# Middle blocks of a five-layer network: deeper lags in the quantised feed-forward, both halves mixed per step in the recurrence, output weights mixed by diagonals on TensorE

## The chip, the cores and the metric

The kernel runs on one core of a Trainium2 chip. The metric is the device time of one execution in microseconds; the figure for a kernel is the median of its runs.

## What is computed

`h` starts as the output of a token attention over looked-up embeddings (16 heads), a spin attention is added to it, and then come the three parts that matter here, cut to their core. `h` has 2 sequences of 1024 tokens, 256 wide.

```python
# L0_ffn: fake-quantised activations and weights, scale from the largest absolute value
xq   = quant(layernorm(h), clip_x)
hid  = quant(silu(xq @ qw(w_gate).T) * (xq @ qw(w_up).T), clip_down)     # 704 wide
h    = h + hid @ qw(w_down).T
# L1_attn: 8 experts' weights are mixed once per sequence, then a gated linear recurrence
u     = layernorm(h)
x     = u * rsqrt(mean(u*u) + 1e-6) * norm_weight
probs = softmax(mean(x, axis=1) @ router_w.T + router_b)                 # [2, 8]
W_hg, W_out = einsum('be,ekd->bkd', probs, w_hg), einsum('be,eod->bod', probs, w_out)
hidden, gate = split(x @ W_hg.T)
state_t = (1 - sigmoid(gate)) * state_(t-1) + sigmoid(gate) * g(hidden)
h    = h + (state @ W_out.T + u)
# L1_ffn: six layers of windowed attention and gated feed-forward on layernorm(h)
h    = h + L1_ffn(layernorm(h))
```

## The kernel before

The program is a row of blocks with a barrier of all engines between them: `attentions` (both attentions and the quantisation of the weights), `feed_forward`, `recurrence`, `local_layers` (six layers, 96 tile steps) and `store_sum`. Only `feed_forward` and `recurrence` are touched by the change. Within a block each engine has a queue of its own whose order is written out by hand, and semaphores tie them together. Tokens are cut into 4 chunks of 512 (`CHUNKS`) and 8 pairs of 128-token tiles (`PAIRS`); PSUM has 8 banks of 128x512 float32.

**`feed_forward`, gates.** VectorE clips `X` in two operations per chunk (`clip_x`, L1515 and L1517), ScalarE rounds it to bf16 (`round_x`, L1453), TensorE turns it (`turn`, L1384), ScalarE takes it back (`take_x`). Then come 6 units per chunk: TensorE makes gate and up (`gate_up`, L1394, three bank pairs), ScalarE applies Silu (`gated`, L1465), VectorE multiplies (`multiply`, L1523) and takes the largest of each half (`largest`, L1530). `clip_x` of chunks 2 and 3 stands inside VectorE's loop, at `j == 4` of chunks 0 and 1. GpSimd first clears the tail of `hT` (L1335), then sets `power` and `ones`.

**`feed_forward`, down projection.** Once the largest value is known, each of 8 pairs `g` goes through this chain: `to_integers` (ScalarE, L1469), `clip_h` (VectorE, L1536), `round_h` (ScalarE, L1474), `down` (TensorE, L1404), `scale_output` (VectorE, L1541), `add_output` (GpSimd, L1346), `count` (VectorE, L1547 and L1550), `deviations` (GpSimd, six small operations), `norm` (VectorE, L1555), `join` (GpSimd, L1367) and `norm_again` (ScalarE, L1482), `turn_normed` with the sums (TensorE, L1414 and L1421), `take_normed` (VectorE, L1560). VectorE's order in step `g` is:

```python
clip_h(g); count(g - 1); scale_output(g); norm(g - 1); take_normed(g - 3)   # and near the end:
mean_of(0)  # at g == 6;   logits(0)  # at g == 7;   shares(0)  # at g == 8
```

After the loop stand `mean_of(1)`, `logits(1)` and `shares(1)`. `shares` also writes `shareT`, the shares times the norm's weight (L1588).

**`recurrence`.** VectorE mixes the gate weights of a unit `n` (sequence, 128 outputs) from 8 experts: `mix(n)` has 16 operations of 128x256, two (k = 0, 1) per expert (L1770, L1773). TensorE multiplies (`hidden_gate(n)`, L1703, 8 float32 matmuls of 512 columns, which the profile shows as 16 records), ScalarE takes three sigmoids (L1742 to L1744), VectorE scans (`scan(n)`, L1778, L1781, L1783), in the order mix 0, 1, 2, scan 0, mix 3, scan 1, 2, 3. The output weights are mixed beside it: ScalarE scales each expert's (`weigh_output`, L1737) and GpSimd adds them up (L1684), 7 additions per sequence. Then TensorE makes the outputs of 8 pairs (`output`, L1718, 4 float32 matmuls of 256 columns each, 8 records), VectorE adds them to `H` (`add_output`, L1789), counts (L1794, L1797) and norms (L1802), with the deviations from GpSimd (L1689, L1691); SyncE writes `H` to memory. The last norm ends the block.

## Time and profile before

| | |
|---|---|
| median of 3 runs | 4301.55 us (4298.23 to 4302.67) |
| the profiled execution | 4291.31 us, span 4289.4 us, mean granted clock 0.969 |
| busy over the span | TensorE 95%, VectorE 73%, ScalarE 63%, GpSimd 46% |
| `feed_forward` | 1076.9 to 1207.0 us of the span |
| `recurrence` | 1207.3 to 1288.4 us |
| `local_layers` | 1289.6 us to 4271 us |

A row of the timeline has its start and length in us, then engine, line, operation, tiles and how many instructions it merges. Busy is the time in which an engine executes; the idle time before a group is put down to what ended it. The granted clock is TensorE's, 1.00 for 2.4 GHz and 0.50 for 1.2 GHz. The shares are those of the whole program, most of which the change does not touch; what it does touch is 211 us long, so it has to be read by stages.

### The profile page before, as it was taken

The numbers are of one execution on the slowest core, as the hardware profiler recorded it, in microseconds if no ns is written. First come the engines' busy times: TensorE is split into PE (matmuls) and PEld (weight loads), VectorE is DVE, ScalarE is ACT, GpSimd is POOL, SyncE is SP. The second block draws the span as 40 slices with busy tenths as digits, with TensorE's granted clock in tenths as the row PEclk, the third lists the DMA queues.
The fourth block names the chain that finished last, engine by engine and source line by source line (L and its number), as shares of the span: only waits on it lengthen the run. The fifth ranks groups of instructions, "written<-read, shape, count | busy, mean of one in ns | idle before, by whom it ended". The sixth has DMA issues, their size and how long they took to land. (4 is left out here: it accounts for less than half of the span.)

```text
span 4289.4 us, 98138 instructions
## 1 busy us (share of the span) xinstructions
PE 4058.3 (95%) x33209; PEld 2830.0 (66%) x33212; DVE 3115.0 (73%) x5389; ACT 2681.0 (63%) x7061; POOL 1969.9 (46%) x1362
## 2 busy tenths in 40 slices
PE   6999979999567999999999999999999999999997
PEld 3666546665234777777777777777777777777776
DVE  4888548887686777777777777677777777777774
ACT  3677536776425666666666666666666666666664
POOL 1000000000235665666665656566656666566662
PEclk8999989999679999999999999999999999999999
DMA  6111142220102000210011101110011100111001
GB/s 156 38 43 44 24 120 65 55 54 15 59 20 92 21 20 19 61 39 21 19 52 41 31 16 24 47 52 18 21 35 44 43 19 21 48 47 25 21 20 49
DMA packets 103319, 177.61 MB, mean 41 GB/s; under 512 B 27317, under 2 KB 61905, under 8 KB 102737
## 3 DMA queue, kind: packets, MB, share of 16 engines
q1 hardware_dynamic: 102096, 169.70, 14.8%
q8 instruction: 256, 4.19, 0.4%
q0 software_dynamic: 768, 2.10, 0.4%
q14 instruction: 199, 1.62, 0.1%
HBM read 94.93 MB, written 23.07 MB: 28 GB/s over the span
## 5 line engine op out<-in xcount | busy, mean ns | idle before, releaser
L2160 POOL TENSOR_TENSOR swp<-raw,table 128x512 f32<-128x512 f32 x384 | 481.1, 1274 | 663.0 <-DVE ss L2571 662.8
L938 DVE TENSOR_REDUCE maxima<-PS 128x1 f32<-128x512 f32 x1024 | 632.4, 681 | 123.7 <-PE PS L772 123.3
L2243 PE MATMUL PS<-wqk,xT 128*128 128x512 f32 x1536 | 688.9, 601 | 5.7 <-DMA wqk<-in_L_ffn_Wqkv 4.4
L2190 POOL TENSOR_TENSOR probs<-probs,prob_recip 128x512 f32<-128x512 f32 x384 | 475.5, 1257 | 432.6 <-DVE prob_recip L2629 432.6
L902 ACT ACTIVATE probs<-PS 128x512 f32<-128x512 f32 x1024 | 520.2, 602 | 154.6 <-PE PS L786 153.9
L2500 ACT ACTIVATE probs<-probs,neg 128x128 f32<-128x128 f32 x1536 | 595.9, 389 | 27.1 <-DVE neg L2623 25.6
L2170 POOL TENSOR_TENSOR rinv<-ssm,power 128x32 f32<-128x32 f32 x96 | 525.8, 5477 | 0.0
L2243 PEld LDWEIGHTS PS<-wqk,xT 128*128 128x128 f32 x1536 | 283.8, 190 | 338.3 <-issue 254.6
L2346 PE MATMUL PS<-xnT,w 128*128 128x128 f32 x3840 | 479.9, 276 | 0.4 <-DVE hidden L2689 0.4
L772 PE MATMUL PS<-k_stack,q_stack 112*128 112x512 f32 (+1 forms) x1024 | 430.6, 442 | 35.4 <-PEq L640 19.9
L2346 PEld LDWEIGHTS PS<-xnT,w 128*128 128x128 f32 x3840 | 455.2, 193 | 1.4 <-issue 0.7
L2571 DVE TENSOR_REDUCE ss<-swp 128x16 f32<-128x1024 f32 x192 | 232.9, 1213 | 305.5 <-ACT swp L2451 305.5
L2450 ACT ACTIVATE raw<-PS 128x512 f32<-128x512 f32 x384 | 229.5, 598 | 283.0 <-PE PS L2243 279.2
L786 PE MATMUL PS<-q_stack,k_stack 128*128 128x512 f32 x1024 | 392.2, 414 | 2.1 <-ACT probs L902 2.1
L756 POOL COPY v_head<-V 128x256 f32 (+1 forms) x64 | 25.1, 401 | 709.1 <-PE PS L797 646.1
L2325 PE MATMUL PS<-wo,oT 128*128 128x256 f32 x1536 | 347.4, 379 | 0.0
L2243 PE MATMUL PS<-wv,xT 128*128 128x512 f32 x768 | 345.8, 593 | 1.2 <-ACT swp L2451 1.2
L2614 DVE TENSOR_TENSOR probs<-PS,maskf 128x512 f32<-128x512 f32 x384 | 261.6, 681 | 102.3 <-PE PS L2287 102.3
L2635 DVE COPY pT<-PS 128x512 f32<-128x512 f32 x192 | 132.7, 691 | 249.9 <-PE PS L2296 249.5
L2473 ACT ACTIVATE kT<-PS 128x512 f32<-128x512 f32 x192 | 115.2, 600 | 308.9 <-PE PS L2261 308.9
L2325 PEld LDWEIGHTS PS<-wo,oT 128*128 128x128 f32 x1536 | 284.4, 190 | 34.7
L772 PEld LDWEIGHTS PS<-k_stack,q_stack 112*128 112x128 f32 (+1 forms) x1024 | 201.3, 197 | 130.8 <-issue 62.4
(275 smaller groups left out, 8210.9 us busy)
## 6 DMA issues: line engine op xcount, KB each, us to landing
V_window<-V SPq DMA_DIRECT2D x180, 256.0 KB, 2.8
wqk<-in_L_ffn_Wqkv SPq DMA_DIRECT2D x12, 1024.0 KB, 6.4
w<-in_L_ffn_W SPq DMA_DIRECT2D x18, 640.0 KB
q_stack<-spin_qk SPq DMA_DIRECT2D x128, 80.0 KB
k_stack<-spin_qk SPq DMA_DIRECT2D x128, 80.0 KB
q_stack<-tok_qk SPq DMA_DIRECT2D x128, 64.0 KB, 2.7
k_stack<-tok_qk SPq DMA_DIRECT2D x128, 64.0 KB, 2.8
spin_qk<-shared SPq DMA_DIRECT2D x32, 256.0 KB
```

Source lines behind the costliest of these rows:

```text
L772: pe.matmul(SM(r, k), qs[0:KMAX, r, q * P:(q + 1) * P], ks[0:KMAX, r, half * CH:(half + 1) * CH], start=True, stop=True).then_inc(sm_done, 1)
L786: pe.matmul(ST(r, k), ks[:, r, (k // 2) * P:(k // 2 + 1) * P], qs[:, r, (k % 2) * CH:(k % 2 + 1) * CH], start=True, stop=True).then_inc(st ...
L902: act.activation(probs[:, k // 2, (k % 2) * CH:(k % 2 + 1) * CH], ST(r, k), ACT.Exp).then_inc(exp_done, 1)
L938: dve.tensor_reduce(maxima[:, k // 2, k % 2:k % 2 + 1], SM(r, k), AX.X, ALU.max).then_inc(sm_maxed, 1)
L2160: pool.tensor_tensor(swp[:, w, :, a:a + LD // 2], raw[:, w, :, b:b + LD // 2], table[:, j % 2, 2 + w, a:a + LD // 2].rearrange("p (o d) -> ...
L2170: pool.tensor_tensor(rinv[:, :], ssm[:, :], power[:, :], ALU.pow).then_inc(S["inv_ready"], 1)
L2190: pool.tensor_tensor(view, view, psr[:, 4 * q:4 * q + 4].rearrange("p (h o) -> p h o", o=1) .to_broadcast([P, 4, P]), ALU.mult).then_inc(p ...
L2243: mm = pe.matmul(wide(kind, half, j), xT[:, k, at:at + P], rhs, start=(k == 0), stop=(k == DC - 1))
L2325: mm = pe.matmul(ATT, oT[:, j % 2, k * P:(k + 1) * P], wo[:, k, :], start=(k == 0), stop=(k == PAIRS - 1))
L2346: mm = pe.matmul(bank[:, at * P:(at + 1) * P], w1[:, w, k, f * P:(f + 1) * P], xnT[:, k, :], start=(k == 0), stop=(k == DC - 1), skip_grou ...
L2500: ins_ = act.activation(probs[:, h, :], src, ACT.Exp, bias=neg[:, h:h + 1], accum_out=psum_[:, h:h + 1])
L2614: dve.tensor_tensor(probs[:, 4 * q:4 * q + 4, :], SC(q % 2), maskf[:, int(j % QT == 0), :].rearrange("p (o k) -> p o k", o=1).to_broadcast ...
```

## The change

- `feed_forward`, gates: `clip_x` of all chunks stands ahead of the loop; GpSimd sets `power` and `ones` before it clears the tail of `hT`; ScalarE begins with one Silu of a single column into a new tile `table`.
- `feed_forward`, down projection: `clip_h` runs one pair ahead; `count(g)` follows in the same step as `scale_output(g)`; `add_output` moves from GpSimd to VectorE; ScalarE's order is `round_h(g + 1)`, `to_integers(g + 2)`, `norm_again(g - 2)`; `turn_normed` and `take_normed` lag by one pair more. `mean_of(0)`, `logits(0)` and logits on TensorE come one step later; `exponentials(0)` and `shares(0)` stand at the very end. `take_normed` multiplies by the norm's weight, in two operations, one per k; `shareT` is gone.
- `recurrence`: `mix` has one operation of 128x512 per expert, over both k; each waits for the one before. The output weights of both sequences are mixed on TensorE (`blend_output`, behind `hidden_gate(0)`), against diagonal matrices that VectorE makes after `mix(0)` (`diagonal`), and ScalarE takes them (`take_blend`). `hidden_gate(1)` waits for both, since it uses the same banks. `weigh_output` and GpSimd's additions are gone. ScalarE begins with a Sigmoid of a single column. The norm at the end moves from VectorE to ScalarE, as `H * rstd - mean * rstd`, whose offset GpSimd makes in two more small operations.

```diff
@@ feed_forward, gpsimd
-                pool.memset(hT[64:P, IC - 1, :], 0.0).then_inc(cleared, 1)
-                pool.wait_ge(cleared, 1)
                 pool.memset(power[:, :], -0.5).then_inc(cleared, 1)
                 pool.memset(ones[:, :], 1.0).then_inc(cleared, 1)
+                pool.wait_ge(cleared, 2)
+                pool.memset(hT[64:P, IC - 1, :], 0.0).then_inc(cleared, 1)
...
                     if g < PAIRS:
-                        add_output(g)
                         deviations(g)
@@ tensor
-                for g in range(PAIRS + 2):
+                for g in range(PAIRS + 3):
                     if g < PAIRS:
                         down(g)
-                    if g >= 2:
-                        turn_normed(g - 2)
-                    if g == PAIRS // BATCH + 2:
+                    if g >= 3:
+                        turn_normed(g - 3)
+                    if g == PAIRS // BATCH + 3:
                         logits(0)
@@ scalar
+                act.activation(table[:, :], c.ident[:, 0:1], ACT.Silu)
                 round_x(0)
...
                 to_integers(0)
+                to_integers(1)
+                round_h(0)
                 for g in range(PAIRS + 2):
                     if g + 1 < PAIRS:
-                        to_integers(g + 1)
-                    if g < PAIRS:
-                        round_h(g)
+                        round_h(g + 1)
+                    if g + 2 < PAIRS:
+                        to_integers(g + 2)
                     if g >= 2:
                         norm_again(g - 2)
-                    if g == PAIRS // BATCH + 3:
-                        exponentials(0)
+                exponentials(0)
                 exponentials(1)
@@ vector
+                def add_output(g):
+                    at = slice(PAIR * g, PAIR * g + PAIR)
+                    dve.wait_ge(out_scaled, g + 1)
+                    dve.tensor_tensor(c.H[:, at, :], c.H[:, at, :], scaled_out[:, g % 2, :, :], ALU.add).then_inc(ffn_added, 1)
...
                     dve.wait_ge(r_turned, g + 1)
-                    dve.tensor_copy(x.RT[:, :, PAIR * g * P:PAIR * (g + 1) * P], c.PS[:, 2 + g % 2, :].rearrange("p (k t) -> p k t", k=DC)).then_inc(r_taken, 1)
+                    for k in range(DC):
+                        ins_ = dve.tensor_scalar(x.RT[:, k, PAIR * g * P:PAIR * (g + 1) * P], c.PS[:, 2 + g % 2, PAIR * k * P:PAIR * (k + 1) * P],
+                                                 nw[:, k:k + 1], None, ALU.mult)
+                    ins_.then_inc(r_taken, 1)
...
-                clip_x(1)
+                for ch in range(1, CHUNKS):
+                    clip_x(ch)
...
-                        if j == 4 and ch + 2 < CHUNKS:
-                            clip_x(ch + 2)
...
-                for g in range(PAIRS + 3):
-                    if g < PAIRS:
-                        clip_h(g)
-                    if 1 <= g <= PAIRS:
-                        count(g - 1)
+                clip_h(0)
+                for g in range(PAIRS + 4):
+                    if g + 1 < PAIRS:
+                        clip_h(g + 1)
                     if g < PAIRS:
                         scale_output(g)
+                        add_output(g)
+                        count(g)
                     if 1 <= g <= PAIRS:
                         norm(g - 1)
-                    if g >= 3:
-                        take_normed(g - 3)
-                    if g == PAIRS // BATCH + 2:
+                    if g >= 4:
+                        take_normed(g - 4)
+                    if g == PAIRS // BATCH + 3:
                         mean_of(0)
-                    if g == PAIRS // BATCH + 3:
+                    if g == PAIRS // BATCH + 4:
                         logits(0)
-                    if g == PAIRS // BATCH + 4:
-                        shares(0)
                 mean_of(1)
                 logits(1)
+                shares(0)
                 shares(1)
@@ recurrence, tensor
+                def blend_output(b):
+                    pe.wait_ge(diag_ready, b + 1)
+                    for k in range(DC):
+                        for e in range(E):
+                            if b == 0 and k == 0:
+                                pe.wait_ge(x.out_loaded[e], 16)
+                            mm = pe.matmul(c.PS[:, 4 + b, k * D:(k + 1) * D], diag[:, b, e, :], x.wout[:, e, k, :], start=(e == 0), stop=(e == E - 1))
+                    mm.then_inc(blended, 1)
...
                 for n in range(len(units)):
                     hidden_gate(n)
+                    if n == 0:
+                        for b in range(BATCH):
+                            blend_output(b)
@@ scalar
+                def take_blend(b):
+                    act.wait_ge(blended, b + 1)
+                    act.activation(x.mixed_out[:, b, :, :], c.PS[:, 4 + b, :].rearrange("p (k d) -> p k d", k=DC), ACT.Copy).then_inc(blend_taken, 1)
+                def norm(ch):
+                    act.wait_ge(shift_done, 4 * ch + 4)
+                    for t in range(4 * ch, 4 * ch + 4):
+                        act.activation(c.X[:, t, :], c.H[:, t, :], ACT.Identity, bias=offset[:, 1, t:t + 1], scale=rstd[:, t:t + 1]).then_inc(normed, 1)
@@ vector
+                        src = x.whg[:, e, :, :].rearrange("p k (w i) -> p k w i", w=2)[:, :, :, o * P:(o + 1) * P]
...
+                            dve.wait_ge(mixed_in, E * n + e)
+                            dve.scalar_tensor_tensor(out=dst, in0=src, scalar=x.share[:, b, e:e + 1], in1=dst, op0=ALU.mult, op1=ALU.add).then_inc(mixed_in, 1)
...
+                def diagonal(b):
+                    dve.tensor_tensor(diag[:, b, :, :], c.ident[:, :].rearrange("p (o f) -> p o f", o=1).to_broadcast([P, E, P]),
+                                      x.share[:, b, :].rearrange("p (e o) -> p e o", o=1).to_broadcast([P, E, P]), ALU.mult).then_inc(diag_ready, 1)
                 mix(0)
+                diagonal(0)
+                diagonal(1)
                 mix(1)
```

## Rows read from the trace of the kernel before

**Rows 1.** Windows: busy us (instructions) by engine, PEclk, DMA share, GB/s; five stages
```profile
1077.00:1128.00 51.00, 31.01 (x125) 12.97 (x128) 37.90 (x44) 24.61 (x33) 2.59 (x4) 0.77 0.37 124
1128.00:1192.00 64.00, 36.70 (x159) 23.04 (x159) 31.29 (x66) 29.66 (x29) 32.65 (x56) 0.55 0.00 1
1192.00:1207.00 15.00, 9.22 (x42) 8.61 (x41) 11.62 (x33) 2.12 (x6) 6.67 (x10) 0.50 0.00 0
1207.00:1269.00 62.00, 35.44 (x80) 16.58 (x80) 57.52 (x77) 23.35 (x29) 21.10 (x15) 0.80 0.00 0
1269.00:1289.60 20.60, 12.58 (x48) 10.16 (x48) 16.53 (x56) 0.00 (x0) 5.30 (x9) 0.84 0.25 102
```

**Rows 2.** Timeline (start us, us, engine line op [idle before <-releaser]), start of `feed_forward`
```profile
1076.88 1.80 POOL L1335 MEMSET hT<- 64x2048 f32 x1 [1.43 <-POOLq L646]
1076.92 2.31 DVE L1515 TENSOR_SCALAR X<-X,shared 128x1024 f32<-128x1024 f32 x1 [1.02 <-PEq L646]
```

**Rows 3.** Gates: a table load (lines by form), then starts of three chunks (timeline)
```profile
L1465 ACT ACT_TABLE_LOAD x1 | 1.3, 1283 | 2.0 <-PE PS L1394 2.0
...
1099.93 1.40 DVE L1523 SCALAR_TENSOR_TENSOR hT<-PS,gu_scale,silu 128x512 f32<-128x512 f32 x2
...
1110.28 1.40 DVE L1523 SCALAR_TENSOR_TENSOR hT<-PS,gu_scale,silu 128x512 f32<-128x512 f32 x2
...
1119.17 1.40 DVE L1523 SCALAR_TENSOR_TENSOR hT<-PS,gu_scale,silu 128x512 f32<-128x512 f32 x2
```

**Rows 4.** Timeline of one step of the down projection; last two rows: lines by form
```profile
1158.07 0.69 DVE L1541 TENSOR_TENSOR scaled_out<-PS,both_scales 128x512 f32<-128x512 f32 x1 [3.81 <-PE PS L1404]
1158.68 1.68 DVE L1555 TENSOR_SCALAR X<-H,moments,rstd 128x256 f32<-128x256 f32 x2
1158.84 1.36 POOL L1346 TENSOR_TENSOR H<-H,scaled_out 128x512 f32<-128x512 f32 x1 [0.61 <-DVE scaled_out L1541]
...
1160.88 0.94 DVE L1536 TENSOR_SCALAR hT<-hT 128x1536 f32<-128x1536 f32 x1
1161.74 0.74 DVE L1547 BATCH_NORM_STATS2 stats<-H 128x6 f32<-128x256 f32 x2
1161.86 1.48 ACT L1474 ACTIVATE hq<-hT 128x1536 bf16<-128x1536 f32 x1 [4.69 <-DVE hT L1536]
...
1163.39 3.08 PE L1404 MATMUL PS<-shared,hq 128*128 128x256 bf16 x12 [2.81 <-ACT hq L1474]
...
L1367 POOL TENSOR_TENSOR H<-H,X 128x512 f32<-128x512 f32 x8 | 10.1, 1264 | 0.0
...
L1550 DVE BATCH_NORM_AGGREGATE moments<-stats 128x2 f32<-128x6 f32 x16 | 2.4, 172 | 0.0
```

**Rows 5.** Timeline, end of `feed_forward`: last output scaled, sums of a pair, end
```profile
1192.47 0.69 DVE L1541 TENSOR_TENSOR scaled_out<-PS,both_scales 128x512 f32<-128x512 f32 x1 [3.81 <-PE PS L1404]
...
1193.27 1.71 PE L1421 MATMUL PS<-ones,R 128*128 128x1 f32 x8
...
1206.63 0.36 DVE L1588 TENSOR_SCALAR share_norm<-share,norm_w 128x8 f32<-128x8 f32 x2
```

**Rows 6.** Timeline, `recurrence`, mixing with and without GpSimd beside it
```profile
1207.85 12.70 DVE L1773 SCALAR_TENSOR_TENSOR mixed_hg<-whg,share_norm,mixed_hg 128x256 f32<-128x256 f32 x14
...
1208.71 9.97 POOL L1684 TENSOR_TENSOR mixed_out<-mixed_out,product 128x512 f32<-128x512 f32 x7 [1.32 <-ACT product L1737]
...
1220.99 5.62 DVE L1773 SCALAR_TENSOR_TENSOR mixed_hg<-whg,share_norm,mixed_hg 128x256 f32<-128x256 f32 x14
```

**Rows 7.** Timeline, `recurrence`: gate and output matmuls, last scan, last norm
```profile
1220.60 19.59 PE L1703 MATMUL PS<-RT,mixed_hg 128*128 128x512 f32 x40 [15.57 <-DVE mixed_hg L1773]
...
1260.75 3.62 PE L1718 MATMUL PS<-mixed_out,hT 128*128 128x256 f32 x16
...
1266.36 2.29 DVE L1783 TENSOR_TENSOR_SCAN hT<-keep,value 128x1024 f32<-128x1024 f32 x1
...
1287.06 1.38 DVE L1802 TENSOR_SCALAR X<-H,moments,rstd 128x256 f32<-128x256 f32 x4 [0.28 <-POOL rstd L1691]
```

More of the change, by code:

```diff
@@ L1274, in __init__ @@
         self.share = c.sb(ctx, "share", [P, BATCH, EXPERTS])
-        self.shareT = c.sb(ctx, "share_norm", [P, BATCH, DC, EXPERTS])
         self.hg_loaded = [c.sem(f"hg_loaded{e}") for e in range(EXPERTS)]
@@ L1287, in feed_forward @@
         hT = c.sb(ctx, "hT", [P, IC, TOK])
+        table = c.sb(ctx, "table", [P, 1])
         silu = c.sb(ctx, "silu", [P, 2, CH])
@@ L1580, in shares @@
                     dve.wait_ge(exped, b + 1)
[L1581 to L1593 removed]
+                    dve.tensor_reduce(one[:, b, 1:2], lg[:, b, 2, :], AX.X, ALU.add).then_inc(route[b], 1)
+                    dve.wait_ge(route[b], 4)
+                    dve.reciprocal(one[:, b, 2:3], one[:, b, 1:2]).then_inc(route[b], 1)
+                    dve.wait_ge(route[b], 5)
+                    dve.tensor_scalar(x.share[:, b, :], lg[:, b, 2, :], one[:, b, 2:3], None, ALU.mult).then_inc(route[b], 1)
+                route = [c.sem("route0"), c.sem("route1")]
                 clip_x(0)
                 dve.tensor_scalar(gu_scale[:, :, :], m.up_scale[:, :, :], m.act_scale[:, 0, 0:1], None, ALU.mult).then_inc(gu_ready, 1)
[L1597 removed]
+                for ch in range(1, CHUNKS):
+                    clip_x(ch)
                 dve.wait_ge(r_loaded, 48)
@@ L1656, in recurrence @@
         rstd = c.sb(ctx, "rstd", [P, TILES])
-        mixed_in, multiplied, summed = c.sem("mixed_in"), c.sem("multiplied"), c.sem("summed")
+        table = c.sb(ctx, "table", [P, 1])
+        offset = c.sb(ctx, "offset", [P, 2, TILES])
+        diag = c.sb(ctx, "share_diag", [P, BATCH, E, P])
+        mixed_in = c.sem("mixed_in")
+        diag_ready, blended, blend_taken, normed = c.sem("diag_ready"), c.sem("blended"), c.sem("blend_taken"), c.sem("normed")
         hg_done, hg_sig, hg_step, scanned = c.sem("hg_done"), c.sem("hg_sig"), c.sem("hg_step"), c.sem("scanned")
         out_done, added, spill_done = c.sem("out_done"), c.sem("added"), c.sem("spill_done")
-        power_set, counted, moments_ready, shift_done, rstd_ready = (c.sem(n) for n in "power_set counted moments_ready shift_done rstd_ready".split())
+        power_set, counted, moments_ready, shift_done = (c.sem(n) for n in "power_set counted moments_ready shift_done".split())
         units = [(b, k) for b in range(BATCH) for k in range(DC)]
@@ L1710, in output @@
                         pe.wait_ge(scanned, DC * b + DC)
-                        pe.wait_ge(summed, (E - 1) * (b + 1))
                     if g < 2:
@@ L1744, in sigmoids @@
                     act.activation(keep[:, n % 2, :], bank(n, 1), ACT.Sigmoid, scale=-1.0).then_inc(hg_sig, 1)
-                for e in range(E):
-                    weigh_output(0, e)
+                act.activation(table[:, :], c.ident[:, 0:1], ACT.Sigmoid)
                 sigmoids(0)
-                for e in range(E // 2):
-                    weigh_output(1, e)
-                sigmoids(1)
-                for e in range(E // 2, E):
-                    weigh_output(1, e)
-                sigmoids(2)
-                sigmoids(3)
+                for b in range(BATCH):
+                    take_blend(b)
+                for n in range(1, len(units)):
+                    sigmoids(n)
+                for ch in range(CHUNKS):
+                    norm(ch)
             @block.vector
@@ L1797, in count @@
                         dve.bn_aggr(moments[:, t, :], stats[:, t, :]).then_inc(moments_ready, 1)
-                def norm(ch):
-                    dve.wait_ge(rstd_ready, ch + 1)
-                    for t in range(4 * ch, 4 * ch + 4):
-                        dve.tensor_scalar(c.X[:, t, :], c.H[:, t, :], moments[:, t, 0:1], rstd[:, t:t + 1], ALU.subtract, ALU.mult)
+                def diagonal(b):
+                    dve.tensor_tensor(diag[:, b, :, :], c.ident[:, :].rearrange("p (o f) -> p o f", o=1).to_broadcast([P, E, P]),
+                                      x.share[:, b, :].rearrange("p (e o) -> p e o", o=1).to_broadcast([P, E, P]), ALU.mult).then_inc(diag_ready, 1)
                 mix(0)
+                diagonal(0)
+                diagonal(1)
                 mix(1)
@@ L1815, in _ @@
                     count(ch)
-                    if ch:
-                        norm(ch - 1)
-                norm(CHUNKS - 1)
 LAYERS = 6
```

67 lines of the change are left out of this document (17 added, 50 removed).

## The prediction

> **What bounds the kernel now.** The change leaves 95% of the program alone, so the engines' shares of the whole span say nothing about it. I first cut the span at the block borders and read the windows [rows 1]: gates (1077 to 1128), down projection (to 1192), its tail (to 1207), recurrence to its last scan (to 1269), outputs (to 1289.6). No engine is busy throughout in the first three: in the down projection TensorE has 36.7, VectorE 31.3, ScalarE 29.7 and GpSimd 32.7 us of 64. That is a chain, not a full engine. In the recurrence VectorE is busy 57.5 of 62 us. Then I read the timeline of each stage for what ends last.
>
> In the gates a chunk takes 10.35 us where a clip stands in VectorE's loop (1099.93 to 1110.28) and 8.89 us where none does (1110.28 to 1119.17) [rows 3]. In the down projection one step takes 8.44 us from one scaled output to the next. The ring in it: `clip_h` at 1160.88, `round_h` at 1161.86, `down` at 1163.39 to 1166.47, the next scaling, then the norm, whose two operations take 1.68 us because GpSimd's addition beside them takes 1.36, then `take_normed`, then the next clip [rows 4]. In the recurrence the first mix takes 13 us (14 operations in 12.70 us) while GpSimd adds output weights; the second, alone, does them in 5.62 [rows 6]. TensorE waits 15.57 us for it [rows 7].
>
> **The sum, part by part.** Gains count as negative. All times are against the profiled execution (4291.31 us, span 4289.4), which lies 10.2 us below the median; I carry the difference over to the median.
>
> *Start.* VectorE's first clip takes 2.31 us, beside GpSimd's clearing of 1.80 us that began 0.04 us earlier [rows 2]. With the two small clearings first, VectorE may get through, or its second operation may wait in the first one's place. Bounds 0 and -1.5; I take the middle, -0.7.
>
> *Gates.* The table load of 1.28 us stands between the first gate and everything behind it (ScalarE waited for TensorE, then loaded) [rows 3]; now it is loaded in the wait for the first clip: -1.3. Two clip pairs leave the loop. Their price is the difference of the two chunks, 1.46 us each: -2.9. Ahead of the loop they are hidden while TensorE turns and multiplies the first unit. The last wait for a late turn goes too, perhaps -0.6. Against it: what VectorE gives up, TensorE may not follow in the first chunk, where its clock is 0.50; I put back 0.4. Sum -4.4, bounds -2.5 and -6.
>
> *Down projection.* With `clip_h` a pair ahead, the ring through TensorE spans two steps. From clip to scaled output it is 5.6 us (0.98 to the rounding, 1.53 to `down`, 3.08, a semaphore); from there to the next clip VectorE does the scaling 0.69, the addition 0.69 (as the scaling, its nearest row), statistics 0.74, aggregation 0.3 (2.4 us over 8 pairs), norm 0.8 (half of 1.68, once nothing stands beside it) and the taking, 0.7 as the scaling [rows 4]: 3.9. So 9.5 us per two steps, 4.8 a step; VectorE's own work with the clip's 0.94 is 4.9 less small overlaps, also 4.8. ScalarE needs 1.5 + 1.5 + 0.9 = 3.9. TensorE needs 3.08 for `down` and, at the low clock, 1.71 for the sums [rows 4, 5] and 0.9 for the turns before them: 5.7. So the next bound is TensorE at 1.2 GHz, 5.7 a step, or VectorE at 4.8. The granted clock in this window is 0.55 [rows 1], but TensorE idles over 40% of it; without the waits it is nearly always busy, and rows 7 show the clock come up in such a stretch. I take 4.9 for the five later steps. The filling: the first scaled output as before, 7.6 us into the stage (1128.6), the second 3.4 later (the second `down` now waits only for the first), the third 4.8 later, then 5 x 4.9: the last at 40.3, where it was at 63.9 (1192.47) [rows 5]: -23.6.
>
> The addition now on VectorE is where a stall can come back. Mixing beside GpSimd's additions took 0.91 us an operation (12.70/14) against 0.40 alone (5.62/14) [rows 6], and `join` on GpSimd, 1.26 us [rows 4], comes due, behind its six small operations for the pair just counted, about when the next addition does. It costs between 0 and 1.26 us a step; within 4.9 only a little of it is in. The Trainium skill (SBUF — State Buffer, "Who interferes with whom") says that a VectorE instruction with two SBUF inputs and a GpSimd instruction that reads SBUF exclude each other for the whole instruction. Rows 6 agree, at 0.91 against 0.40. By that rule every step in which the two meet would be up to 1.26 us longer; the case has a place among the rivals.
>
> *Tail.* Before, 14.5 us from the last scaled output to the end (1192.47 to 1206.99) [rows 5]. Now a turn more is left on TensorE: its sums of pair 4 wait for `mean_of(0)`, which stands behind VectorE's addition, count, norm and taking, 4.5 us after the last scaling. Then 1.8 for them, 1.0 for the logits, and three pairs of 2.7 at the low clock or 1.9 at the high one, and 3.6 for the rest as before (`shareT`'s 0.36 gone, `shares(0)` in its place): 19 or 16. I take 17.1: +2.6. Down projection and tail: -21.0, bounds -15 (low clock throughout) and -27.
>
> *Recurrence to the last scan.* The first mix becomes one operation of 0.5 and seven of about 0.73 (0.40 from start to start at 256 columns, alone [rows 6]; 0.27 for as many again at a column a VectorE cycle, by my estimate; 0.06 for the wait on the one before, which it now always has): 5.6 us instead of 13.2. Without GpSimd beside them the later mixes are 5.6 too. So VectorE's 57.5 us shrink to 4 x 5.6 for mixes, 4 x 4.8 for scans and 2 x 1.2 for the diagonals, 44, and TensorE becomes the bound. Its chain from the first mix: 5.6, the first gates 9.1 (40 records in 19.59 us [rows 7] are 5 or 6 of 0.85 at the low clock and the others of 0.43, so 16 from cold are 9.1), then the blends. These are new: 32 float32 matmuls of 256 columns, and the nearest row has 8 of the same kind in 3.62 us (16 records) [rows 7]: 14.0. They end at 28.7, ScalarE takes the second in 0.7, then three gates of 16 x 0.43 = 6.9: 50.1. Three sigmoids, 3.0, and a scan of two operations of 1.2 and one of 2.29 [rows 7], 4.8: 57.9. Before it was 61.3 (1207.3 to 1268.65) [rows 7]: -3.4. So of 7.6 us saved in the mix, and more later, the blends eat most. Bounds -1 (the gates start cold again behind the 0.7 us wait) and -6 (blends at 11).
>
> *Outputs.* The norms leave VectorE, whose chunk shrinks from 4.2 to 2.9 us, but each chunk then waits for TensorE, 3.6 us, which starts cold after waiting for the last scan, as now. The last count ends 1.4 us sooner; behind it GpSimd has two small operations more (0.6), and the norm of four tiles on ScalarE takes 1.8 where VectorE took 1.38 [rows 7]. -0.4, bounds +1 and -2. The writing of `H` starts behind the additions, so ahead of the last count, and I leave it out.
>
> Sum: -0.7 - 4.4 - 21.0 - 3.4 - 0.4 = -29.9. 4301.55 - 29.9 = 4271.6, say 4272 us. Nothing goes to `local_layers`, whose code and data are the same.
>
> **The rivals.**
> - *TensorE bounds the down projection at 1.2 GHz.* For it: 0.55 granted there, and the window after it 0.50. Against: the gaps that go. Then 5.7 a step and 19 in the tail: the gain there is 15 instead of 21, in all 24: 4278 us.
> - *`join` meets VectorE's addition in every step.* For it: rows 6. Against: with a longer step the two drift apart. 8 steps of 6.0 instead of 4.9 or 4.8: 9 us back, 4281 us.
> - *The blends don't pay.* If they run at the low clock, or the gates behind them start cold, the recurrence is 7 to 10 us later than I have it and a little slower than before: 4280 us. For it: window 0.80 in rows 1. Against: TensorE has no gap before them.
> - *Slower: the clock stays at 1.2 GHz from the first gate of the recurrence on.* Then gates 13.7 each and blends 27.4: 5.6 + 13.7 + 27.4 + 0.7 + 3 x 13.7 + 7.8 = 96 instead of 61, +35, and the gain before it is only 18: +17, 4318 us. It decides once 30 of the some 39 us that I count at the high clock run at the low one. Rows 7 speak against it: 40 records in 19.59 us can't be all low.
> - *The change doesn't do what it says:* a hidden order (GpSimd's `join`, ScalarE's `norm_again` behind the next pair's work) holds the ring at one pair, 8.4 a step. Then only 9 us are left, with a longer tail: 4292 us.
>
> **The numbers.** Forecast 0.62, low clock 0.14, `join` 0.08, blends 0.08, no pipelining 0.06, slower 0.02. The range takes the bounds together, -16 to -42 with some room for the spread of the runs (4 us): 4258 to 4287; this leaves out the last two and tails of the others. About 0.2%, 8.6 us, can be told from no change. Faster 0.93, same 0.05, slower 0.02.
>
> **What would show it.** Right: the table load at 1077; chunks of 8.2 to 8.9 us; outputs scaled 4.8 to 5 us apart with the granted clock above 0.7; 16 to 19 us behind the last; the first mix in 5.6 us; 32 blend matmuls in 14 us with VectorE waiting for sigmoids before scan 1; the block's end on ScalarE. Wrong: steps over 5.6 us with VectorE idle on TensorE, or an addition of 1.5 us or more instead of 0.69; blends over 20 us, or a difference behind 1290 us of the span.

## The result and the profile after

The kernel after takes 4246.04 us (median of four, 4245.33 to 4248.83), beside 4299.89 us for the kernel before (4295.53 to 4302.67): ratio 0.9877, 95% interval 0.986 to 0.9894. The forecast of 4272 us, with its range from 4258 us up, was too high: the kernel is faster than the range allowed. The profiled execution took 4245.51 us (span 4243.6, mean granted clock 0.975), 45.8 us less than that of before.

Where the 45.8 us lie, from marks in both timelines (us of the span):

| stretch | before | after | difference | forecast |
|---|---|---|---|---|
| ahead of `feed_forward` | 1076.88 | 1078.35 | +1.5 | 0 |
| `feed_forward` to the last maximum | 50.5 | 43.9 | -6.6 | -5.1 |
| from there to the first mix | 79.9 | 61.1 | -18.9 | -21.0 |
| first mix to the end of the last scan | 61.33 | 59.9 | -1.4 | -3.4 |
| outputs and the border behind them | 20.9 | 20.7 | -0.3 | -0.4 |
| `local_layers`, to the last tile's last addition | 2980.0 | 2959.7 | -20.2 | 0 |

The two blocks that were changed gave 27.2 us, against 29.9 in the forecast. The rest came in `local_layers`, where no line was touched. The 1.5 us ahead of `feed_forward` are spread from run to run: over all profiled runs here that block begins between 1076.3 and 1086.6 us, in kernels that are the same up to there.

The windows of the kernel after by stage, which answer to [rows 1] (gates, down projection, its tail, recurrence, outputs):

```profile
1078.35:1123.00 44.65, 27.99 (x128) 11.21 (x128) 38.03 (x45) 24.68 (x34) 2.83 (x4) 0.84 0.42 142
1123.00:1164.00 41.00, 33.36 (x143) 20.70 (x143) 33.30 (x71) 28.02 (x28) 26.23 (x43) 0.50 0.00 1
1164.00:1183.00 19.00, 12.71 (x59) 11.73 (x57) 11.33 (x41) 3.88 (x8) 7.91 (x13) 0.59 0.00 0
1183.00:1243.00 60.00, 48.31 (x144) 28.32 (x144) 43.67 (x46) 14.10 (x16) 0.11 (x1) 0.89 0.00 1
1243.00:1263.80 20.80, 12.29 (x48) 10.25 (x48) 12.02 (x41) 8.30 (x16) 6.84 (x16) 0.85 0.25 101
```

The down projection went from 64 to 41 us with nearly the same work on TensorE (143 matmul records instead of 159, since one turn more is left for the tail), and its clock was 0.50 to the end. From 1143 to 1164 us TensorE has no gap at all:

```profile
1143.00:1164.00 21.00, 21.00 (x95) 15.01 (x94) 19.76 (x42) 14.07 (x17) 17.65 (x29) 0.50 0.01 1
```

In the recurrence VectorE fell from 57.5 to 43.7 us and TensorE rose from 35.4 to 48.3: the bound has changed hands.

Now the stretch that no line of the change explains. TensorE's timeline of the kernel before at the first turn of the layer loop of `local_layers`:

```profile
2208.62 0.66 PE L2296 MATMUL PS<-ident,probs 128*128 128x128 f32 x4
2211.96 1.11 PE L2296 MATMUL PS<-ident,probs 128*128 128x128 f32 x4 [2.68 <-issue]
2212.86 1.92 PE L2346 MATMUL PS<-xnT,w 128*128 128x128 f32 x8
```

and of the kernel after at the same place:

```profile
2182.90 1.09 PE L2298 MATMUL PS<-ident,probs 128*128 128x128 f32 x8
2183.83 1.06 PE L2348 MATMUL PS<-xnT,w 128*128 128x128 f32 x8
```

The first four of these matmuls end one pass of the loop and the next four begin the next one (a "turn" is this border). Before, 2.68 us lie between them in which TensorE waits for nothing that the profile knows ("issue"); after, nothing. Then its clock has fallen. Windows of the kernel before at this turn (the columns as in rows 1):

```profile
2209.00:2212.00 3.00, 0.32 (x4) 0.09 (x2) 2.61 (x7) 0.00 (x0) 3.00 (x1) 0.91 0.02 5
2212.00:2215.00 3.00, 3.00 (x15) 3.00 (x16) 0.32 (x1) 1.88 (x3) 3.00 (x3) 0.53 0.00 0
```

Eight matmuls that take 1.06 us after take 1.92 here. The last additions of two neighbouring tiles, which stand 30.3 to 30.8 us apart everywhere else but for the last five, are 34.8 us apart at this turn, and 36.0, 35.0 and 34.9 at the next three; after, they are 30.5 at all of them. That makes 18.7 of the 20.2 us.

### The profile page after: what moved, and what is told of

It reads as the page before. It is cut to its first block and busy times, and to the rows that moved or that the text cites. A ratio compares the mean times of both kernels' runs of the same rounds, so it can differ in the third digit from the quotient of the medians.

```text
span 4243.6 us, 98196 instructions
## 1 busy us (share of the span) xinstructions
PE 4058.3 (96%) x33276; PEld 2832.9 (67%) x33276; DVE 3098.7 (73%) x5355; ACT 2679.4 (63%) x7065; POOL 1954.0 (46%) x1348
## 5 line engine op out<-in xcount | busy, mean ns | idle before, releaser
L2502 ACT ACTIVATE probs<-probs,neg 128x128 f32<-128x128 f32 x1536 | 595.9, 389 | 27.2 <-DVE neg L2625 25.7
```

Of the source, the lines that this page charges most:

```text
L2502: ins_ = act.activation(probs[:, h, :], src, ACT.Exp, bias=neg[:, h:h + 1], accum_out=psum_[:, h:h + 1])
```

## The experiments

My theory: the wait is TensorE fetching instructions at the loop's back edge, and whether it shows depends on where the loop's code happens to lie. The mixing by diagonals adds 32 float32 matmuls, which are 64 matmul and 64 weight-load instructions, and two waits to TensorE's code ahead of the loop: 130 instructions. Rival A: the wait comes from timing, DMA traffic or tile addresses, which the change moves too. Rival B concerns the recurrence: VectorE's mixing sets the pace of the gates.

In each run below "the turns" are the intervals at the four turns of the loop, "the layers" the time from the first tile's last addition to the 96th (2819.6 us before, 2799.2 after), `feed_forward` runs from its clearing of `hT` to the first mix (130.4 and 104.6), and the recurrence from there to the next block's first transfer (82.3 and 80.6). These come from one profiled execution of each run. Where its code was not changed, `feed_forward` took 128.7 to 131.1 us in the runs that have it as before and 102.7 to 104.8 in those that have it as after, so a difference of 2 us in it says nothing by itself.

### e1 and e2: moving the code, and nothing else

```diff
                 for g in range(PAIRS):
                     output(g)
+                for _ in range(130):          # 126 in e2, in the kernel after
+                    pe.sem_inc(padded, 1)
```

Expected of e1: 

> The kernel before with 130 TensorE semaphore increments, which do nothing, behind the last output matmul of recurrence, so that TensorE's code of local_layers lies as far back as in the kernel after (128 matmul and weight-load instructions and two waits more). Theory (instruction fetch at the back edge of the layer loop): the intervals of 34.8 to 36.0 us at the loop turns go to 30.5, local_layers gets 20 us shorter and the whole 13 to 20 us shorter (the increments may cost up to 7 us in recurrence): 4280 to 4287 us. Rival A (the stall comes from timing, DMA traffic or tile addresses that recurrence leaves): the intervals stay at 34.8 to 36 us and the time at 4300 to 4307 us.

Expected of e2: 

> The kernel after with 126 such increments in the same place: 130 + 126 = 256, one whole block of instructions, so that the layer loop lies in its block as in the kernel before. Theory: the long intervals come back (34.8 to 36 us at four loop turns), local_layers is 20 us longer, the whole 4266 to 4273 us. Rival A: intervals stay 30.5 us and the time 4246 to 4253 us.

e1: 4284.25 us beside 4292.62, ratio 0.9984 (0.9975 to 0.9994). The turns are 30.5 us, the layers 2801.1; the increments themselves cost 11.4 us in the recurrence (93.7), more than the 7 allowed. e2: 4274.14 us, ratio 0.9952 (0.9936 to 0.9969). The turns are 35.2, 35.3, 36.6 and 35.3, the layers 2820.9; the whole is 1 us over the expected range, which had left out what the increments cost (the recurrence takes 90.6 us, 10.0 more). The wait is back in the kernel after, in the same place (TensorE's timeline of e2):

```profile
2191.27 0.66 PE L2301 MATMUL PS<-ident,probs 128*128 128x128 f32 x4
2194.79 0.65 PE L2301 MATMUL PS<-ident,probs 128*128 128x128 f32 x4 [2.86 <-issue]
```

So instructions that do nothing take the stall out of the kernel before and put it into the kernel after. Rival A falls: e2 has the tiles and the transfers of the kernel after and e1 those of before, and but for the 10 to 11 us of the increments the timing too; e3 and e4 below need no increments at all. And 130 + 126 = 256 instructions bring the old state back. The Trainium skill ("Runtime: NRT & Kernel Launch", section "Instruction fetch mechanics") says that instructions are fetched in blocks of 256, or 16 KiB. The trace agrees: the DMA view of the kernel before from 2205 to 2213 us has two transfers of together 0.03 MB on the instruction queue.

```profile
q8 instruction: 2, 0.03, 1.7%
```

### e3, e4, e10, e11, e14, e15: which places stall

The loop's first instruction can be put on a chosen slot of a block, for TensorE alone:

```diff
-            with eng.Fori(1, LAYERS) as l:
+            with nc.Fori(1, LAYERS, engines=bass.OrderedEngineSet([eng.engine]),
+                         head_slot={eng.engine: 0} if eng is nc.tensor else None) as l:
```

e4, e10, e11 and e14 have 64, 176, 224 and 239 there. e15 is e1 with 20 increments. All are the kernel before otherwise.

Expected of e3: 

> The kernel before with TensorE's layer loop begun on slot 0 of a 256-instruction block, nothing else. Theory: the size of the intervals at the loop turns depends on the slot alone; 30.5 us (whole 4280 us) or 34.8 and more (4300 us), and the entry from the unrolled first layer may cost some us. Rival A: no change, 4300 us and 34.8 to 36 us.

Expected of e4: 

> The same with the loop begun on slot 64. Theory: as for slot 0, and a value other than there would show that the slot decides. Rival A: no change, 4300 us and intervals of 34.8 to 36 us.

Expected of e10: 

> The kernel before with TensorE's layer loop begun on slot 176 of its 256-instruction block (slots 0 and 64 were without long intervals). If the loop of the kernel before happens to begin near here, or if the stall comes wherever few instructions are left in the block behind the loop's head, the intervals at the loop turns are 34.8 us and more; otherwise 30.5 us.

Expected of e11: 

> The same with slot 224: 31 instructions are left in the block behind the loop's head. If a short rest of a block is what makes TensorE wait, this one has the longest intervals of all (35 us or more at the turns); if only one narrow place stalls, 30.5 us.

Expected of e14: 

> The kernel before with TensorE's layer loop begun on slot 239: 16 instructions are left in the block behind the loop's head. If the wait at the back edge is TensorE's having run through that rest before the next block is there, it is longer than the 1.1 us that slot 224 showed: intervals of 32.5 to 35 us at the loop turns. If the slot itself decides in some other way, 30.5 or 31.6 us as for slot 224.

Expected of e15: 

> The kernel before with 20 increments on TensorE behind recurrence's last output matmul. If the loop of the kernel before begins just short of a block's end, 20 instructions move its head over the end, and the intervals go to 30.5 us. If the stall has a wide range of places, they stay at 34.8 to 36 us.

| run | head of the loop | turns, us | layers, us | time, us |
|---|---|---|---|---|
| e3 | slot 0 | 30.5, four times | 2801.5 | 4274.08 (ratio 0.9957, 0.9941 to 0.9973) |
| e4 | slot 64 | 30.5, four times | 2800.0 | 4274.63 (0.9958, 0.9942 to 0.9974) |
| e10 | slot 176 | 30.7, 30.7, 30.5, 30.5 | 2801.9 | 4276.55 |
| e11 | slot 224 | 31.8, 31.5, 31.5, 31.7 | 2805.6 | 4279.46 |
| e14 | slot 239 | 35.8, 32.3, 34.3, 34.5 | 2816.0 | 4288.71 |
| e15 | 20 further than before | 30.5, four times | 2801.6 | 4273.49 |

e10, e11, e14 and e15 are one execution each. e11 missed: I expected the longest intervals of all and it has 1.1 us more per turn. But the rows say why. TensorE's timeline of e11, then of e14, at the first turn:

```profile
2210.35 1.09 PE L2296 MATMUL PS<-ident,probs 128*128 128x128 f32 x8
2211.28 1.06 PE L2346 MATMUL PS<-xnT,w 128*128 128x128 f32 x8
2212.17 0.27 PE L2350 MATMUL PS<-xnT,w_tail 128*106 128x128 f32 x1
2213.58 0.49 PE L2350 MATMUL PS<-xnT,w_tail 128*106 128x128 f32 x3 [1.14 <-issue]
```

```profile
2209.63 1.09 PE L2296 MATMUL PS<-ident,probs 128*128 128x128 f32 x8
2210.56 0.39 PE L2346 MATMUL PS<-xnT,w 128*128 128x128 f32 x2
2213.25 1.65 PE L2346 MATMUL PS<-xnT,w 128*128 128x128 f32 x6 [2.31 <-issue]
```

The loop begins at the fifth matmul of the first row. With 32 instructions from the head to the block's end (e11) TensorE runs 13 matmuls of the loop and then waits 1.14 us; with 17 (e14) it runs 6 and waits 2.31; in the kernel before it runs none and waits 2.68. A matmul here is two instructions, its weight load and itself, so 26 and 12, and the others are waits and increments. In all three the wait ends 2.7 to 3.1 us after the head was passed (half of the first row's 1.09 us: 2210.9 to 2213.58, 2210.2 to 2213.25; before, 2209.28 to 2211.96). That fits one rule: the block behind the head's comes about 3 us after TensorE has passed the head, and the rest of the head's block is all that it has until then. With 80 instructions left (e10) it is hidden but for 0.2 us.

The trace has the branch and the transfers too. In the kernel before, the loop's own line at the first turn shows (durations in ns), and the DMA view of the wait, 2209.3 to 2211.9 us, has one transfer, of instructions:

```profile
L1961 PEldq COMPARE_BRANCH  x1: 3686/3686/3686, 2205.0 to 2205.0; - x1
```

```profile
q8 instruction: 1, 0.02, 2.8%
```

The branch begins at 2205.0 us, while TensorE still has 4.3 us of matmuls queued ahead of it, and lasts 3.69 us. At the end of the last pass, where the loop is left, it lasts 0.08. A block of instructions (16384 bytes) is transferred from 2206.37 us on, within the branch, and the next from 2209.44 us on for 1.16 us, within the wait, which ends 1.36 us after that. It is so in every run, with the wait and without it: one such transfer begins 0.9 to 1.6 us behind a taken branch and the next 4.0 to 5.4 us behind it (at five turns one more begins within 0.4 us of the branch). The first I take for the head's block and the second for the one behind it, by their order; the trace doesn't name them. So the head's block has to be fetched as well, and the queued matmuls hide it; the next one begins some 3 us later, and it is hidden only by what is left of the head's block. The smaller waits of e6 to e8 below are of another kind, and stand at these five turns alone: at the first of e6 two transfers ran beside each other right behind the branch, the second took 2.04 us, the branch 4.60, and TensorE waited 0.59 us at the loop's first matmul.

The same section of the Trainium skill says that a taken branch to a block that isn't held forces a fetch before execution can go on. The trace agrees: 3.3 to 4.6 us for a taken branch over all runs, with a transfer inside it, and 0.08 us for one not taken.

The slot on which the loop of the kernel before begins stands in no row; that its head stands within 20 instructions of a block's end, as e15 suggests, is inferred from the above.

### e5 and e6: each half of the change alone

e5 is the kernel after with `recurrence` of the kernel before, which takes `x.share[:, b, e:e + 1]` for `shareT`. e6 is the kernel before with `recurrence` of the kernel after and this edit of `take_normed`:

```diff
-dve.tensor_copy(x.RT[:, :, PAIR * g * P:...], c.PS[:, 2 + g % 2, :]...)
+for k in range(DC):
+    dve.tensor_scalar(x.RT[:, k, PAIR * g * P:...], c.PS[:, 2 + g % 2, ...], nw[:, k:k + 1], None, ALU.mult)
```

Expected of e5: 

> The kernel after with recurrence as before (it takes the share directly, since the norm's weight already lies in RT). TensorE's code ahead of the layer loop is as long as before. Theory: feed_forward ends 24 us earlier (from its first instruction: 127 us to 103 to 105), recurrence stays at 82 us, and the long intervals of local_layers stay (34.8 to 36 us, four of them), so the whole is 24 to 26 us shorter: ratio 0.994. Rival A (earlier timing or other tile addresses cured the layers): intervals 30.5, 44 to 46 us shorter, ratio 0.989.

Expected of e6: 

> The kernel before with recurrence as after, and with it only the edit of feed_forward that it needs (RT is written with the norm's weight). Theory: feed_forward within 1 us of before, recurrence 1.5 to 2 us shorter, and the long intervals gone, since the 128 matmul and weight-load instructions of the mixing shift the loop: 20 to 22 us shorter, ratio 0.995. Rival A: intervals stay 34.8 to 36 us, 1 to 3 us shorter, ratio 0.9995. Between this run and the last the gain of the change (54 us) should divide into 25 and 21, with the rest from run to run.

e5: 4269.01 us, ratio 0.9942 (0.9926 to 0.9959). `feed_forward` 103.4, recurrence 82.6, turns 35.0, 36.4, 35.3 and 34.8, layers 2819.6. e6: 4272.71 us, ratio 0.9952 (0.9936 to 0.9969). `feed_forward` 131.9, recurrence 79.7, turns 31.3, 31.1, 30.5 and 30.5, layers 2803.1. So what is in `feed_forward` is worth 26 to 27 us, the recurrence 2.6, and the shift of code 17. The new `take_normed` costs about 0.9 us of it: from the first rounding of `hT` to bf16 to the last scaled output e6 takes 61.9 us and all other runs with this order 60.9 to 61.2. (I had expected less than 1 us more for `feed_forward` and 1.5 to 2 us for the recurrence, and missed both by little.) The halves add up, 24.0 + 20.3 = 44.3 us by the medians beside 4293.02, against 45.8 for the profiled pair. The 54 us by which the medians of the first comparison differ are not reached; there the kernel before had 4299.89 us, and 4291 to 4297 us beside the later runs. The larger part of what the new recurrence "brings" is where it leaves the code of another block.

### e7, e8: the mixing of the output weights elsewhere

```diff
 # e7: no blend behind the first gate; banks 2 and 3, free once the third gate's sigmoids are done
-                    if n == 0:
-                        for b in range(BATCH):
-                            blend_output(b)
                 for g in range(PAIRS):
+                    if g % (PAIRS // BATCH) == 0:
+                        blend_output(g // (PAIRS // BATCH))
                     output(g)
 # e8: instead of this
+                blend_output(0)                 # ahead of hidden_gate(0); diagonal by ScalarE
                 for n in range(len(units)): hidden_gate(n)
                 for g in range(PAIRS):
+                    if g == 2: blend_output(1)
                     output(g)
```

The other engines follow: in e7 ScalarE takes the mixings behind all sigmoids and VectorE makes the diagonals behind the third mix, in e8 sequence 1's alone.

Expected of e7: 

> The kernel after with the two mixings of the output weights taken out from behind the first gate and put ahead of the outputs that read them: sequence 0's behind the last gate, sequence 1's ahead of output 4, in PSUM banks 2 and 3. Theory (the matmuls of recurrence are one chain on TensorE from the first gate to the last, 10.2 + 14.0 + 20.8 us, so the 14.0 us of mixing sit on the path and nothing hid them): the last scan ends 12 to 14 us earlier (from the first mix: 59.9 to 46 to 48 us), and the outputs give back 8 to 10 of it, for TensorE now has them beside the mixing: net 3 to 6 us, 4240 to 4243 us. Rival B (VectorE's mixing sets the pace of the gates, so TensorE had room behind the first gate, as the change supposes): the last scan moves by under 3 us and the whole gets slower by 8 us or more.

Expected of e8: 

> The same, but sequence 0's mixing is put ahead of the first gate, while VectorE still mixes the gates' weights and TensorE is idle (ScalarE writes its diagonal), and sequence 1's behind output 1. Theory: the first gate ends 1 to 3 us later than in the kernel after (its matmuls find the clock risen), the last scan 10 to 12 us earlier, outputs lose 1 to 3 us: net 7 to 10 us, 4236 to 4240 us. Rival B: the last scan moves by under 3 us.

e7: 4244.44 us, ratio 0.989 (0.9874 to 0.9907), 1 us over the expected range and not told apart from the kernel after. The last scan ends 49.0 us after the first mix instead of 59.9 (10.9 earlier, where I expected 12 to 14), so Rival B falls: TensorE had no room behind the first gate. But the outputs take 29.6 us instead of 20.7, since each mixing stands ahead of the outputs that read it and VectorE waits for them. The timeline of e7 has sequence 1's mixing, and then VectorE's fifth addition, 7.19 us late:

```profile
1236.78 7.07 PE L1699 MATMUL PS<-wout,share_diag 128*128 128x256 f32 x32
1246.59 0.69 DVE L1791 TENSOR_TENSOR H<-PS,H 128x512 f32<-128x512 f32 x1 [7.19 <-PE PS L1725]
```

e8: 4237.09 us, ratio 0.9872 (0.9855 to 0.9888). The last scan ends 47.9 us after the first mix and the outputs keep their 20.7, so the recurrence lasts 68.6 us instead of 80.6. Sequence 0's mixing runs while VectorE mixes the first gates; the first gates then need 7 us, not 10.2, since the clock has come up, and sequence 1's mixing lies beside the last sigmoids and scan. The timeline of e12, whose recurrence is that of e8:

```profile
1182.55 5.88 DVE L1781 SCALAR_TENSOR_TENSOR mixed_hg<-whg,share,mixed_hg 128x512 f32<-128x512 f32 x7
1184.44 8.83 PE L1700 MATMUL PS<-wout,share_diag 128*128 128x256 f32 x32 [4.52 <-ACT share_diag L1759]
1193.10 20.76 PE L1713 MATMUL PS<-RT,mixed_hg 128*128 128x512 f32 x48
...
1215.03 7.11 PE L1713 MATMUL PS<-RT,mixed_hg 128*128 128x512 f32 x16 [1.17 <-DVE value L1786]
...
1225.43 4.91 PE L1700 MATMUL PS<-wout,share_diag 128*128 128x256 f32 x22
```

### e9: the pace of the down projection

```diff
                         for k in range(DC):
+                            if 0 < t % QT < QT - 1 and not (i == PAIR - 1 and k == DC - 1):
+                                continue
                             mm = pe.matmul(c.PS[:, 4 + k, 0:1], R[...], ones[:, 0:1], ...)
```

Expected: 

> The kernel after without 9 of every 16 one-column matmuls that add up the normed rows for the router (its shares are then of other means). In the kernel after, seven steps of the down projection last 5.46 us at the end, and TensorE's rows in one of them are 3.06 + 1.11 + 1.70 us with no gap at a granted clock of 0.50. Theory (TensorE at 1.2 GHz sets this pace, not VectorE, whose own rows come to 5.0 us): the steps fall to 5.0 to 5.1 us and the last scaled output comes 1.5 to 3 us earlier than 41.35 us behind the first rounding; if the clock rose too, more. Rival (VectorE or the lock between it and GpSimd sets the pace): steps stay at 5.3 to 5.5 us.

A single run, 4241.13 us. The expectation is off in one point: not seven but the last three of the seven steps of the kernel after last 5.46 us. The scaled outputs of the kernel after, from the fifth on, and then those of e9 (timelines):

```profile
1148.38 0.69 DVE L1536 TENSOR_TENSOR scaled_out<-PS,both_scales 128x512 f32<-128x512 f32 x1
1153.84 0.69 DVE L1536 TENSOR_TENSOR scaled_out<-PS,both_scales 128x512 f32<-128x512 f32 x1
1159.30 0.69 DVE L1536 TENSOR_TENSOR scaled_out<-PS,both_scales 128x512 f32<-128x512 f32 x1 [0.76 <-PE PS L1398]
1164.76 0.69 DVE L1536 TENSOR_TENSOR scaled_out<-PS,both_scales 128x512 f32<-128x512 f32 x1 [0.61 <-PE PS L1398]
```

```profile
1143.60 0.68 DVE L1538 TENSOR_TENSOR scaled_out<-PS,both_scales 128x512 f32<-128x512 f32 x1
1148.50 0.69 DVE L1538 TENSOR_TENSOR scaled_out<-PS,both_scales 128x512 f32<-128x512 f32 x1
1153.41 0.68 DVE L1538 TENSOR_TENSOR scaled_out<-PS,both_scales 128x512 f32<-128x512 f32 x1
1158.31 0.68 DVE L1538 TENSOR_TENSOR scaled_out<-PS,both_scales 128x512 f32<-128x512 f32 x1
```

Steps of 5.46 us become steps of 4.90, at a clock of 0.50 in both. The last scaled output comes 39.1 us after the first rounding instead of 41.35. Not all of this is due to the edit: 0.8 us is there at the third output already, behind 3.4 us at a clock of 1.00 (from 1134.3 us on), which the kernel after was not granted and e2 and e12, without the edit, were.

The clock alone does the same. e2 and e12 have `feed_forward` as the kernel after, with all sums, and were granted 1.00 for 6.8 us in the middle of the down projection. Windows of e2:

```profile
1144.60:1151.40 6.80, 5.16 (x41) 3.83 (x41) 6.62 (x16) 5.66 (x6) 6.14 (x11) 1.00 0.00 0
```

There TensorE has gaps again, the steps from the third output on are 4.8 to 4.9 us but for the last (5.3), and the last scaled output comes at 39.6 us, in e2 as in e12. e7, e8 and e13 were not granted it and have 5.46 and 41.36 us. So where TensorE stays at 1.2 GHz it sets the pace, and VectorE sets it at 4.9 us where TensorE has less to do or the higher clock; which of the two a run gets is worth 1.7 us and was not the same in all.

### e12 and e13: the better version

e12 is e8 with the loop's head on slot 64; e13 is the kernel after itself, on the same chip.

Expected of e12: 

> The kernel of e8_blend_split with TensorE's layer loop begun on slot 64, so that no edit ahead of it can bring the stall back. Expected: no interval over 31 us in local_layers, and a time within 3 us of e8_blend_split: 4233 to 4240 us, which is 7 to 12 us under the kernel after on the same chip. If e8 owed part of its time to where its own loop fell, this one is slower than 4240 us.

Expected of e13: 

> The kernel after itself, for the comparison on this chip: 4243 to 4249 us.

e12: 4233.57 us (4232.91 to 4236.35), ratio 0.9853 (0.9837 to 0.987). e13: 4244.97 us (4244.14 to 4249.4), ratio 0.9878 (0.9861 to 0.9894). The two differ by 11.4 us and their runs don't overlap; the recurrence of the profiled ones takes 68.6 and 79.8 us, and the layers 2800.9 and 2800.8. Fixing the slot costs nothing that can be seen, and where e8 still had 31.1 and 31.2 us at two turns (and e7 31.3 at one, e6 31.3 and 31.1, with TensorE's code ahead of the loop as long as in the kernel after), e12 has 30.5 at all four.

## Why the prediction was wrong

**The step that failed** is the last one of the sum: "Nothing goes to `local_layers`, whose code and data are the same." The code is the same but 130 instructions further on in TensorE's stream, and that was worth 20.2 us of 45.8. I had the sign of it in the text ("a difference behind 1290 us of the span") and no term for it. The intervals of the 96 tiles in the trace of before would have shown four waits on "issue" of 2.6 to 2.7 us, at the loop's turns alone, and so that 19 us hung on something other than the kernel's lines. Without it the blocks of the change give 27.2 us, and 4301.55 less 27.2 is 4274 us (4276 with the 1.5 us ahead of them), inside the range; with it 4301.55 less 45.8 is 4256 us, below its lower end of 4258. The rest of the distance of the medians (54 us) is that the profiled execution of before is 8.6 us below the median of its runs. That the sum over the two changed blocks came within 3 us of the forecast is in part luck: the gates gave more than forecast, and the down projection, its tail and the recurrence less.

**Start:** forecast -0.7, found 0. The first clip fell to 0.76 us, and the second met the clearing in its place, as the worse bound had it. Timeline of the kernel after, which answers to [rows 2]:

```profile
1078.66 2.23 POOL L1338 MEMSET hT<- 64x2048 f32 x1
1079.18 2.26 DVE L1513 TENSOR_SCALAR X<-X 128x1024 f32<-128x1024 f32 x1
```

**Gates:** forecast -4.4, measured -6.6 with the start. The chunks last 8.09 and 8.10 us, not 8.9, against [rows 3] (timeline of the kernel after):

```profile
1097.83 1.40 DVE L1519 SCALAR_TENSOR_TENSOR hT<-PS,gu_scale,silu 128x512 f32<-128x512 f32 x2
...
1105.92 1.40 DVE L1519 SCALAR_TENSOR_TENSOR hT<-PS,gu_scale,silu 128x512 f32<-128x512 f32 x2
...
1114.02 1.40 DVE L1519 SCALAR_TENSOR_TENSOR hT<-PS,gu_scale,silu 128x512 f32<-128x512 f32 x2
```

Even against the chunk of before that had no clips, 8.89 us, each is 0.8 us shorter. VectorE's eight operations in it come to 7.8 us, with two waits of 0.3 us for ScalarE, so "perhaps -0.6" for late turns, over all chunks, was too small.

**Down projection:** the mechanism was right and one term off. The last scaled output came at 41.35 us, forecast 40.3. I took 4.9 us a step, VectorE's pace, because I counted on the high clock for a TensorE without gaps, from [rows 7]. It had no gap for 21 us and was granted 0.50 throughout. e9, e2 and e12 show both: VectorE's pace is 4.90, and 5.46 is TensorE's (3.06 + 1.11 + 1.70 us in rows, less overlaps, and 5.7 in the first rival). So the rival "TensorE bounds the down projection at 1.2 GHz" is what happened, at a smaller price than its 6 us, since the filling was faster than the steps. With the higher clock for 6.8 us, as in e2 and e12, the last scaled output would have come at 39.6 us, so 40.3 lies between the two. The tail took 18.2 us instead of 17.1. VectorE's addition met `join` in one step at full price and in others not, as the middle case had it:

```profile
1159.93 1.27 POOL L1362 TENSOR_TENSOR H<-H,X 128x512 f32<-128x512 f32 x1
...
1160.03 1.72 DVE L1542 TENSOR_TENSOR H<-H,scaled_out 128x512 f32<-128x512 f32 x1
```

In the other seven steps the addition took 0.69 us.

**Recurrence:** forecast -3.4, measured -1.4. The first mix took 6.5 us (0.49, then seven in 5.88), not 5.6: from start to start an operation of 512 columns takes 0.86 us here and 0.79 in the later mixes, where I had 0.73. The first gates took 10.2 instead of 9.1; this one varies with the moment at which the clock rises (8.6 in e13). The blends took what I had, and stand on the path, as I had them. Timeline of the kernel after, which answers to [rows 6] and [rows 7]:

```profile
1183.87 5.88 DVE L1777 SCALAR_TENSOR_TENSOR mixed_hg<-whg,share,mixed_hg 128x512 f32<-128x512 f32 x7
...
1189.81 10.21 PE L1711 MATMUL PS<-RT,mixed_hg 128*128 128x512 f32 x16 [8.58 <-DVE mixed_hg L1777]
...
1199.85 13.98 PE L1698 MATMUL PS<-wout,share_diag 128*128 128x256 f32 x64
...
1214.61 20.84 PE L1711 MATMUL PS<-RT,mixed_hg 128*128 128x512 f32 x48 [0.78 <-ACT mixed_out L1741]
```

**Outputs:** forecast -0.4, measured -0.3. The slower rival did not come near: with the gates warm, 20.84 us for 48 records, the clock was 1.00 from 1199.8 us on. (Its price has a slip: the gain ahead of the recurrence is 20 us by the numbers of the first rival, 0.7 + 4.4 + 15, not 18, which makes it 4316 us.)

## What to carry to other kernels

Before a change is credited with a gain, compare the stages it does not touch: here 20 of 46 us came from where a loop's code lay, could be had in the kernel before by placing the loop's head alone (e3, 18.5 us), and could be lost again by the next edit. A loop whose body is long should have its head pinned where many instructions of its block are left (here slots 0 and 64 were free of the wait, 224 and 239 were not), and small waits on "issue" right behind a back edge are the sign to look for. And work put behind a gate is hidden only if that engine is not the one that sets the stage's pace after the change: the 14 us of mixing paid off ahead of the first gate and beside the last scan, not where the engine had become the bound.

## What was not expected of the hardware

- A taken branch at the end of the layer loop lasted 3.3 to 4.6 us, one not taken 0.08. The transfer of one block of instructions began 0.9 to 1.6 us behind it and that of the next 4.0 to 5.4 us behind it. TensorE's queued matmuls, 4.3 us of them, hid the first but for 0.4 to 0.6 us at five turns of e6, e7 and e8; the second was in time only where enough instructions of the head's block were left. The wait of 2.6 to 2.7 us in the kernel before then cost 4.4 to 5.5 us per turn, for the granted clock fell to 0.50 behind it and eight matmuls took 1.92 instead of 1.06 us.
- TensorE had matmuls under way in 21.00 of 21.00 us with a granted clock of 0.50 throughout. Its work there were 256-column bfloat16 matmuls, 128-column turns and one-column sums. In the recurrence float32 matmuls of 512 columns, which began at 0.50 after a wait of 8.58 us, had it at 1.00 before the first 16 records were done. Which part of the work in the down projection kept it low stays open: e9 took out over half of the one-column sums, and it stayed at 0.50 in these steps, while e2 and e12 had 1.00 for 6.8 us with all of them.
- 130 semaphore increments on TensorE stand 0.15 us apart in e1, 19.9 us in all. 8.5 us of this lay beside the last outputs, and 11.4 us made the block longer.
